# A key bias in linear attention: one TensorE product per key tile, or one more VectorE operation

## The reference, cut to what matters

```python
q = _heads(hidden_states @ q_w.T + q_b, b, s)
k = _heads(hidden_states @ k_w.T + k_b, b, s)
v = _heads(hidden_states @ v_w.T + v_b, b, s)
qp = jax.nn.elu(q) + 1.0
kp = jax.nn.elu(k) + 1.0
kv = jnp.einsum('bhsd,bhse->bhde', kp, v)
z = jnp.einsum('bhsd,bhd->bhs', qp, kp.sum(axis=2))[..., None]
attn = jnp.einsum('bhsd,bhde->bhse', qp, kv) / (z + EPS)
```

## Time and profile before

| | |
|---|---|
| median of 3 runs | 1165.73 us |
| the profiled execution | 1165.65 us |
| its span, first to last instruction | 1162.8 us |
| granted TensorE clock, mean share of full speed | 0.998 |
| TensorE busy | 1127.7 us |
| VectorE busy | 705.3 us |
| ACT busy | 435.6 us |
| GpSimd busy | 358.1 us |

### The profile page before, as it was taken

How to read it: one execution, slowest core, us unless ns; L and a number is a source line. 1 busy time by engine, 2 the same in 40 slices (tenths; PEclk the granted TensorE clock), 3 DMA queues, 4 the chain that set the end, 5 groups by cost and what they waited for, 6 DMA issues and landing times.

```text
span 1162.8 us, 16680 instructions
## 1 busy us (share of the span) xinstructions
PE 1127.7 (97%) x6692; PEld 531.1 (46%) x6718; DVE 705.3 (61%) x1035; ACT 435.6 (37%) x729; POOL 358.1 (31%) x331
## 2 busy tenths in 40 slices
PE   4899999999999999999999999999999999999998
PEld 2344444454444444445444444444454444444443
DVE  4788988776779677996768979677432211111111
ACT  4668788776645251424323324233142200000000
POOL 1000100002126283547525637356332211111111
PEclk9999999999999999999999999999999999999999
DMA  7940233113204541312213213031121325445441
GB/s 268 322 135 1 87 109 110 38 37 109 74 1 143 182 145 74 109 73 78 82 35 118 72 72 118 35 118 43 64 92 48 147 104 179 172 173 176 177 154 59
DMA packets 52236, 125.93 MB, mean 108 GB/s; under 512 B 5216, under 2 KB 15456, under 8 KB 47040
## 3 DMA queue, kind: packets, MB, share of 16 engines
q1 hardware_dynamic: 52160, 124.87, 30.9%
HBM read 77.15 MB, written 47.71 MB: 107 GB/s over the span
## 4 chain that ended last, share of the span: by engine, by line
PE 83%; DVE 7%; issue 4%; ACT 3%; POOL 1%; DMA 1%; SPq 0%; POOLq 0%; DVEq 0%; ACTq 0%
PE bank L1232 26%; PE bank L1234 25%; PE bank L1233 25%; PE bank L1240 2%; DVE look_buf L995 2%; PE bank L1384 1%; DVE w_ffn L995 1%; DMA w_ffn<-in_wmod 1%; PE bank L1302 1%; PE bank L1366 1%; PE bank L1345 1%; DVE h L901 1%; ACT h L617 1%; ACT shared L649 1%; DVE shared L1014 0%
## 5 line engine op out<-in xcount | busy, mean ns | idle before, releaser
L1232 PE MATMUL bank<-h,w_ffn 128*128 128x512 f16 (+1 forms) x528 | 200.6, 380 | 0.2 <-POOL h L553 0.2
L1233 PE MATMUL bank<-h,w_ffn 128*128 128x512 f16 (+1 forms) x528 | 200.3, 379 | 0.0
L1234 PE MATMUL bank<-h,w_ffn 128*128 128x512 f16 (+1 forms) x528 | 200.3, 379 | 0.0
L573 POOL TENSOR_TENSOR shared<-hid_f,shared 128x512 f16<-128x512 f32 (+1 forms) x88 | 114.1, 1296 | 273.5 <-ACT shared L780 273.4
L780 ACT ACTIVATE shared<-hid_f 128x512 f16<-128x512 f32 (+1 forms) x88 | 55.4, 630 | 259.7 <-DVE hid_f L1157 251.8
L1164 DVE SCALAR_TENSOR_TENSOR shared<-bank,sc,gb_row 128x512 f32<-128x512 f32 x32 | 24.0, 751 | 205.1 <-PE bank L1234 205.1
L1157 DVE SCALAR_TENSOR_TENSOR hid_f<-bank,sc,shared 128x512 f32<-128x512 f32 (+1 forms) x88 | 65.8, 747 | 121.5 <-issue 82.4
L1232 PE MATMUL bank<-w_ffn 128*128 128x512 f16 x320 | 121.5, 380 | 0.0
L1234 PE MATMUL bank<-w_ffn 128*128 128x512 f16 x320 | 121.3, 379 | 0.0
L1233 PE MATMUL bank<-w_ffn 128*128 128x512 f16 x320 | 121.3, 379 | 0.0
L1232 PE MATMUL bank<-arena,h 128*128 128x512 f16 x256 | 98.3, 384 | 5.6 <-issue 2.5
(11 more groups left out here) (225 smaller groups left out, 1922.8 us busy)
## 6 DMA issues: line engine op xcount, KB each, us to landing
hid_dram<-shared SPq DMA_DIRECT2D x80, 256.0 KB, 2.0
w_ffn<-hid_dram SPq DMA_DIRECT2D x8, 2560.0 KB, 9.5
xg<-in_x SPq DMA_DIRECT2D x16, 1024.0 KB, 7.2
qp_dram<-qp SPq DMA_DIRECT2D x8, 1024.0 KB, 4.9
x_dram<-xg SPq DMA_DIRECT2D x8, 1024.0 KB, 4.0
xg<-x_dram SPq DMA_DIRECT2D x8, 1024.0 KB, 4.8
out<-xg SPq DMA_DIRECT2D x7, 1024.0 KB, 11.4
qp<-qp_dram SPq DMA_DIRECT2D x6, 1024.0 KB, 5.2
```

Of the source, the lines that this page charges most:

```text
L573: pool.tensor_tensor(hid[0:m, e % HIDS, 1], hid_f[0:m, e % 2], hid[0:m, e % HIDS, 0], ALU.subtract).then_inc(hid_done, 1)
L1232: pe.matmul(dst, a_hi, b_hi, start=first, stop=False)
L1233: pe.matmul(dst, a_hi, b_lo, start=False, stop=False)
L1234: last = pe.matmul(dst, a_lo, b_hi, start=False, stop=end)
```

## The change

The bias is no longer a matmul. VectorE reads each key tile out of PSUM, scales it and adds the bias row (new `k_bias(g, t)`) into a float32 tile `k_t` in SBUF; ACT and the second VectorE operation read `k_t`. TensorE's next use of the bank waits for `k_read`, the new read, and no longer for `kp_done`. The set-up of the three parts and four memsets on GpSimd go. There is one `k_t`, so `k_bias(g, t)` waits for `kp_out` of the tile before. Its place on VectorE is the head of slot o = 2t + 1, except tile 0 of group 0, which is done during set-up.

```diff
             def k_acts(g, t):
-                act.wait_ge(proj_done, OUTS * g + 2 * t + 1 + 2 * OUTS)
+                act.wait_ge(k_read, 4 * g + t + 1)
                 act.wait_ge(kp_done, 4 * g + t + 4)
-                act.activation(k_e, bank[2 + 2 * t % 4][:], ACT.Relu, scale=k_neg_scale, bias=1.0).then_inc(k_neg, 1)
+                act.activation(k_e, k_t, ACT.Relu, scale=-1.0).then_inc(k_neg, 1)
                 act.wait_ge(k_neg, 4 * g + t + 1)
                 act.activation(k_e, k_e, ACT.Exp, scale=-1.0).then_inc(k_act, 1)
...
-            def k_bias():
-                ...
-                then(dve.tensor_scalar(k_neg_scale, c1(C_INV_K), -1.0, None, ALU.mult))
-                then(dve.scalar_tensor_tensor(k_pos_scale, c1(C_INV + S_H1), 2.0 ** 21, c1(C_INV + S_K), ALU.mult, ALU.mult))
-                then(dve.tensor_scalar(k_e, kb_row[:], 1.0, k_pos_scale, ALU.add, ALU.mult))
-                then(dve.tensor_copy(kb_parts, k_e))
-                for rows in (slice(2 * HEAD, 4 * HEAD), slice(3 * HEAD, 4 * HEAD)):
-                    then(dve.tensor_tensor(k_e[rows], k_e[rows], kb_parts[rows], ALU.subtract))
-                    then(dve.tensor_copy(kb_parts[rows], k_e[rows]))
-                dve.sem_inc(kb_ready, 1)
+            def k_bias(g, t):
+                dve.wait_ge(proj_done, OUTS * g + 2 * t + 1 + 2 * OUTS)
+                dve.wait_ge(kp_done, 4 * g + t + 4)
+                dve.scalar_tensor_tensor(k_t, bank[2 + 2 * t % 4][:], c1(C_INV_K), kb_row[:], ALU.mult, ALU.add).then_inc(k_read, 1)
...
-            k_bias()
+            dve.wait_ge(rows_in, 2 * 16)
+            k_bias(0, 0)
...
             def kp_out(g, t):
...
-                dve.scalar_tensor_tensor(kp[:, t % 2], bank[2 + 2 * t % 4][:], c1(C_INV_K), k_e, ALU.mult, ALU.max).then_inc(kp_done, 1)
+                dve.scalar_tensor_tensor(kp[:, t % 2], k_t, 1.0, k_e, ALU.add, ALU.max).then_inc(kp_done, 1)
...
                 for o in range(OUTS):
+                    if o < 2 * TILES and o % 2 == 1 and (g or o > 1):
+                        k_bias(g, o // 2)
                     if o in (2, 4, 6, 8):
                         kp_out(g, o // 2 - 1)
...
                 elif o % 2 == 0:
-                    pe.wait_ge(kp_done, 4 * g + (o - 4) // 2 + 5)
+                    pe.wait_ge(k_read, 4 * g + (o - 4) // 2 + 1)
...
-                is_key = o < 2 * TILES and o % 2 == 0
-                if g == 0 and o == 0:
-
-                    for k, pair in enumerate(pairs):
-                        pe.wait_ge(h_done, 4 + k + 1)
-                        three(bank[2][:], [pair], k == 0, False)
-                    return
                 for k, pair in enumerate(pairs):
                     if o == 0:
                         pe.wait_ge(h_done, 4 * g + 4 + k + 1)
-                    last = three(bank[2 + o % 4][:], [pair], k == 0, k == KC - 1 and not is_key)
-                if g == 0 and o == 1:
-                    pe.wait_ge(kb_ready, 1)
-                    pe.wait_ge(consts, 1)
-                    pe.matmul(bank[2][:], kb_ones, kb_parts, start=False, stop=True).then_inc(proj_done, 2)
-                    return
-                if is_key:
-                    last = pe.matmul(bank[2 + o % 4][:], kb_ones, kb_parts, start=False, stop=True)
+                    last = three(bank[2 + o % 4][:], [pair], k == 0, k == KC - 1)
                 last.then_inc(proj_done, 1)
```

More of the change, by code:

```diff
@@ L30 @@
 F16 = mybir.dt.float16
-BF16 = mybir.dt.bfloat16
 U32 = mybir.dt.uint32
@@ L173, in adaln_kernel @@
         kp = part(shared, 2 * v_w, F32, 2, HID)
-        kb_at = 2 * v_w + 2 * HID
-        kb_parts = shared[:, kb_at:kb_at + HID // 2].bitcast(BF16)
-        kb_ones = shared[:, kb_at + HID // 2:kb_at + HID // 2 + P // 2].bitcast(BF16)
-        k_neg_scale, k_pos_scale = (part(shared, kb_at + HID // 2 + P // 2 + i, F32, 1, 1)[:, 0] for i in range(2))
+        k_t = part(shared, 2 * v_w + 2 * HID, F32, 1, HID)[:, 0]
         k_e = part(shared, 2 * v_w + 3 * HID, F32, 1, HID)[:, 0]
@@ L252, in adaln_kernel @@
         xT_done, h_f_done, h_done, proj_done = sems("xT_done h_f_done h_done proj_done")
-        kb_done, kb_ready, k_neg, k_act, kp_done, v_read = sems(
-            "kb_done kb_ready k_neg k_act kp_done v_read")
+        k_read, k_neg, k_act, kp_done, v_read = sems(
+            "k_read k_neg k_act kp_done v_read")
         q_neg, q_read, q_act, qp_done, qp_out = sems("q_neg q_read q_act qp_done qp_out")
@@ L518, in _ @@
             link(pool.memset(half, -0.5))
-            link(pool.memset(kb_ones, 0.0))
-            for i in (0, 2, 3):
-                link(pool.memset(kb_ones[HEAD * i:HEAD * i + 1], 1.0))
             pool.memset(v_one[:, :, :, HEAD:HEAD + 1], 1.0).then_inc(consts, 1)
@@ L879, in mod_scale @@
                     link(dve.tensor_scalar(modm[:, 2 * i + w], src[:, w], c1(C_SPLIT), None, ALU.mult))
-            def k_bias():
-                def then(ins):
-                    kb_step[0] += 1
-                    ins.then_inc(kb_done, 1)
-                    dve.wait_ge(kb_done, kb_step[0])
-                kb_step = [0]
-                dve.wait_ge(rows_in, 2 * 16)
-                then(dve.tensor_scalar(k_neg_scale, c1(C_INV_K), -1.0, None, ALU.mult))
-                then(dve.scalar_tensor_tensor(k_pos_scale, c1(C_INV + S_H1), 2.0 ** 21, c1(C_INV + S_K), ALU.mult, ALU.mult))
-                then(dve.tensor_scalar(k_e, kb_row[:], 1.0, k_pos_scale, ALU.add, ALU.mult))
-                then(dve.tensor_copy(kb_parts, k_e))
-                for rows in (slice(2 * HEAD, 4 * HEAD), slice(3 * HEAD, 4 * HEAD)):
-                    then(dve.tensor_tensor(k_e[rows], k_e[rows], kb_parts[rows], ALU.subtract))
-                    then(dve.tensor_copy(kb_parts[rows], k_e[rows]))
-                dve.sem_inc(kb_ready, 1)
+            def k_bias(g, t):
+                dve.wait_ge(proj_done, OUTS * g + 2 * t + 1 + 2 * OUTS)
+                dve.wait_ge(kp_done, 4 * g + t + 4)
+                dve.scalar_tensor_tensor(k_t, bank[2 + 2 * t % 4][:], c1(C_INV_K), kb_row[:], ALU.mult, ALU.add).then_inc(k_read, 1)
             def h_lo_a(n, par, c):
```

## The result

The changed kernel takes 1167.39 us (median of 20 runs, 1166.58 to 1169.19) and the kernel before, measured beside it, 1164.41 us (20 runs, 1163.09 to 1167.41). The ratio is 1.0026, with a 95% interval of 1.002 to 1.0032: slower by 3 us, where the forecast said no change (1165.5 us). Its profiled execution took 1166.81 us, 1.16 more than that of before, and its span is 1164.9 us, 2.1 more than the 1162.8 of before. The 0.9 us between the two differences lie outside the span, and this repeats: in all 20 executions of the changed kernel 1.8 to 2.3 us lie outside it (mean 2.0), and in all 66 of the kernel before that the later runs were held against 2.6 to 2.9 (mean 2.8). No run shows what they are.

What follows compares the result with a forecast made beforehand. TensorE, busy 97%, bounds the kernel, with VectorE nearly full in group 2. TensorE loses 9.2 us of work at most, but waits hand it back: places sum to -0.1 us from 1165.65, giving 1165.5 us; range 1160.0 to 1170.0.

Steps and rivals of the forecast that it cites:

- 6: groups 3, 4: Groups 3 and 4: eight bias matmuls go, -1.72 us, less waiting at each first `kv_a`; -1.2 us.
- 7, 8, 9: groups 5, 6: Group 5, tiles 0 to 2: -0.65 us; group 5 to 6: +1.5; group 6, tiles 1 to 3: -0.65.
- place 3: Group 0 to 1: `k_bias(0, 3)` behind lookups makes ACT late, so TensorE waits for `h_lo_a`: +1.55 us.
- place 5: Group 2: VectorE has no idle time, its chain lengthens and TensorE's wait grows to 3.3 us: +2.4 us.
- place 8: Group 5 to 6: late `k_bias(5, 3)` delays ACT and the chain to `qs_all`, where TensorE waits: +1.5 us.
- Place 1: Set-up: TensorE's idle gap goes, -2.54 us; VectorE's `kp_out(0, 0)` is then about as late as `kv_a(0, 0)`, +0.15.
- What would show it: The prediction's list of expected signs, including waits near 1.5 us (group 1), 3.3 (group 2) and 3 (`qs_all`).
- first rival: TensorE stays the bound throughout, so the whole 9.2 us come: 1156.4 us; chance 0.10.
- absorbed delay: ACT's late start at groups 0 to 1 and 5 to 6 is taken up by idle time: 1162.5 us; chance 0.19.
- Place 10: Group 7: TensorE's wait for `m_cut` swallows two biases, one counts: -0.2 us; stage B starts as before.
- The prediction's own sign: If a group other than those named as changing is longer, a chain was missed.
- slower rival: Lower TensorE clock after waits in groups 1 and 2 and before group 6, 1.7 us each: 1170.6 us; chance 0.16.

Runs made afterwards that it cites:

- reb_after: Changed kernel with the table lookups of groups 1 to 5 spread evenly over the 60 slots: 1160.28 us, ratio 0.9958 against the kernel before.
- kb3_early: Changed kernel with `k_bias(0, 3)` and `k_bias(5, 3)` moved ahead of the lookups of slot 6: 1165.67 us, ratio 1.0004 against the kernel before.
- pe_alone: Kernel before without the 32 bias matmuls and their set-up, nothing added to VectorE, key bias missing: 1159.58 us, ratio 0.996.
- delay_g7: Kernel before with one unused VectorE operation of `k_bias`'s form ahead of the lookups in slot 7 of group 7: 1164.31 us, ratio 1.0005.
- kb73_late: Changed kernel with `k_bias(7, 3)` behind the lookups of slot 7, directly before `kp_out(7, 3)`: 1167.57 us, ratio 1.0024 against the kernel before.
- kt_psum: Changed kernel with `k_t` in PSUM bank 7 instead of SBUF: 1166.05 us, ratio 1.0021 against the kernel before.
- kb_after2: Kernel before with the first bias matmul put off until after o = 2 of group 0: 1165.73 us, ratio 1.0004.
- act_first: Changed kernel with ACT reading the bank itself and `k_bias` directly ahead of `kp_out`: 1168.63 us, ratio 1.0039 against the kernel before.
- even_kb3: Changed kernel with evenly spread lookups in groups 1 to 5 and early `k_bias(0, 3)` and `k_bias(5, 3)`: 1159.64 us, ratio 0.995 against the kernel before.
- reb_before: Kernel before with the table lookups of groups 1 to 5 spread evenly over the 60 slots: 1161.13 us, ratio 0.9973.

## Why the prediction was wrong

The forecast's sum by its own places, against the two profiled executions (groups from the table; a boundary falls at a group's fourth `kv_a`):

| places | forecast | measured |
|---|---|---|
| 1, 2: start and group 0 | -2.8 | -2.98 |
| 3, 4: group 1 | +1.5 | +1.59 |
| 5: group 2 | +2.4 | +2.30 |
| 6: groups 3, 4 | -1.2 | -1.40 |
| 7, 8, 9: groups 5, 6 | +0.2 | +0.26 |
| 10: group 7 | -0.2 | +1.72 |
| stage B and later | 0 | +0.57 |
| sum | -0.1 | +2.06 |

**Places 1 to 9** are right within 0.2 us by the groups of the table, and for 3, 5 and 8 so is the mechanism: the chain through ACT in place 3 (TensorE's wait for `h_lo_a` 1.36 us where 1.55 stood), the full VectorE of place 5 (3.13 where 3.3 stood), `qs_all` in place 8 (2.92 where 3.1 stood). Place 1 fits here by luck: the changed kernel's execution came to the set-up 1.5 us earlier, which the change has no part in, and lost 1.5 us there to the lower clock. The waits named under "What would show it" are all there. reb_after shows the cause of 5 by taking it away, kb3_early that of 3 and in part that of 8 (the wait for `qs_all` falls from 2.9 to 2.2 us). Against the first rival pe_alone decides; against the absorbed delay, kb3_early.

**Place 10 failed.** It had -0.2 us, and 1.72 were measured, 1.9 of the 2.2 us by which the forecast's sum misses the two traces. "Stage B starts as before" was said with only `x1_tile` checked. The prediction's own sign for it came true: a group other than those named is longer, so a chain was missed. Two things were missed. `k_bias(7, 3)` moves VectorE's lookups over GpSimd's `xn_b`, on which TensorE's first transposes of stage B wait: 3.21 us became 4.61, and TensorE's wait 1.58. delay_g7 shows the displacement by itself (3.92 us and +0.53), kb73_late takes 0.47 back. And `kp_out` now reads two SBUF sources: I priced it at 0.694 us by line 970, which had run twice, without asking what GpSimd does beside the 32 new ones. 30 of them kept the price (0.70 us at most); the one beside `qn_lo` took 1.64, the one beside `xn_b` 0.87, and that one cost GpSimd 0.7. kt_psum takes both away, and with them 1.51 us of group 7. It leaves 48.32 against 48.11 us, where -0.2 was forecast; the displaced lookups and TensorE's wait of 0.9 us for `xn_b` are in that.

**The base was off**, and this makes about as much of the miss as place 10. The sum was made against an execution of 1165.65 us, called 0.08 under the median. Over 20 runs the median is 1164.41, and the changed kernel's execution is 0.6 under its own median, so the two executions differ by 1.2 us of time and the medians by 3.0. As a sum: 2.06 us in the span, less 0.90 outside it, which the forecast had at nothing, plus 1.24 and 0.58 for where the two executions lie against their medians. By medians, as an estimate from the mean times outside the span (2.0 and 2.8 us), the change costs 3.7 us in the span and gives back 0.75 outside.

The traces show what varies in before. Its profiled execution is one with the late start (`kv_a(0, 0)` at 45.53; 44.35 in delay_g7, where TensorE was at half clock from 34 to 37 us and then idle only 0.86 us in the set-up gap, not 2.54), and the clock at `z_sum` was low in it and full in delay_g7's and kb_after2's, with group 6 at 46.99 against 45.58. Two stretches of delay_g7, against the earlier trace rows:

```profile
266.00:270.00 4.00, 3.15 (x70) 1.91 (x71) 0.76 (x2) 3.97 (x10) 0.00 (x0) 1.00 0.97 295
270.00:274.00 4.00, 3.95 (x22) 1.69 (x24) 1.48 (x3) 2.13 (x7) 1.40 (x3) 1.00 1.03 391
```

The prediction also took a difference of 3.5 us for the least that could be told from no change. With 20 runs of each kernel the interval is 0.7 us either way, and the 3.0 us are clear of it.

**The slower rival** has something in it, but not at the places that it named. It asked for a lower clock after each of three longer waits. At the start of group 1 it never fell (waits of 1.3 to 1.4 us). After the wait in group 2 (3.1 to 3.3 us) it fell in kb73_late and act_first, and not in the changed kernel, kt_psum and kb3_early. At `z_sum`, where the prediction kept the old wait's price in the base and charged one more, it was low in all six traces with a wait of 1.6 to 2.9 us, and in two of the seven with 1.2 or less (before, even_kb3). These are the changed kernel's two stretches, against the earlier trace rows:

```profile
266.00:270.00 4.00, 2.11 (x62) 1.65 (x63) 1.26 (x3) 3.97 (x9) 0.86 (x1) 0.88 0.90 267
270.00:274.00 4.00, 4.00 (x27) 1.67 (x20) 2.18 (x4) 3.50 (x10) 0.19 (x1) 0.70 1.02 390
```

(0.12 + 0.30) x 4 is 1.7 us. The Trainium skill, "TensorE: Matmul & The Clock Gate", Part 1, says that an array left idle is handed 1.2 of its 2.4 GHz; the counts at `z_sum` agree with it (six of six against two of seven), and those in group 2, with the longest wait and the clock mostly full, don't: the length of the wait does not decide it alone. Nor do the other waits of 2 us and more: the clock fell after 2.14 us at `kv_a(0, 0)` in kb_after2 and after 2.09 us in group 1 in act_first, and stayed full after the set-up gap of 2.54 us in before and 2.33 in reb_before. That the changed kernel pays this at `z_sum` and before mostly doesn't could account for most of the gap between a loss of 1.2 us and one of 3.0, beside before's late start; it fits the thirteen traces, but no run took the clock away by itself, so it is not shown.

What stays open: why `z_sum`'s clock differs between executions of kernels that wait about as long there (1.15 to 1.18 us in before, kb_after2, delay_g7 and reb_after, with a fall in before alone), what the 0.75 us outside the span are, and 0.57 us after stage A, where before's profile stands alone (814.11) and kb_after2, with the same code, has 814.44.

## What to carry to other kernels

Work taken from the busiest engine is worth its time only where no other chain is as long: ask of each wait already in the trace, however short, what will be late there once this engine comes sooner. Work added to an in-order engine is priced by its neighbours: what is queued behind it, who waits for that, and which engine works on SBUF at that moment. Before the change is given up, see whether the receiving engine's load can be laid out evenly; here the bias on VectorE, a loss of 3.0 us, became a gain of 0.9 over the bias on TensorE with equally even lookups, and with two small moves one of 4.7. And before a sum of tenths is made, see where its base lies: the one profiled execution of before was 1.2 us above its median.

## What the runs showed of the hardware

VectorE and GpSimd slow each other in some pairings. `scalar_tensor_tensor` 128x512 f32 with two SBUF sources took 1.64 us beside GpSimd's subtraction and 0.69 alone; with one source in PSUM it took 0.74 in the same place. In the other direction GpSimd's `tensor_scalar` 128x512 took 1.50 us beside VectorE's lookups and 1.44 to 1.47 beside the SBUF form of `kp_out` (in five traces), 0.76 to 0.77 beside the PSUM form and where VectorE stood idle. By itself the source hardly matters: the new `kp_out` has a median of 691 ns with k_t in SBUF and 691 in PSUM. TensorE's clock after a wait of 3 us differed between executions of the same instructions in the same place: full in the changed kernel, and fallen at a cost of 1.7 us in kb73_late, whose instructions up to there are the same.
